# A fused graph-network and feed-forward kernel: the dense stage joined, with router work moved behind the sums and the last evictions on VectorE

## The chip, the core and the metric

The kernel runs on one core of a Trainium2 chip. A core has TensorE (PE in the profile: matrix products, results in PSUM), VectorE (DVE), ScalarE (ACT), GpSimd (POOL) and SyncE (SP, which here issues transfers between HBM and the on-chip SBUF). Each engine takes its own instructions in order; they meet by semaphores. The metric is device time in microseconds (us) of one execution, lower is better.

## The reference, cut to what matters

There are 3125 nodes with 256 features, 50000 edges sorted by destination, and two layers. Each layer is a graph step and a feed-forward step, each on the layer-normed rows, added back. The stage of this case computes the end of the first graph step, the whole first feed-forward step, and the start of the second graph step:

```
# end of graph step 0: agg and denominators are already summed per node
msgs = where(deg > 0, agg, V)                  # 3125 x 256, four heads
y    = msgs @ Wo + bo + h                      # h: the normed node rows
x    = x + layernorm(y) * gamma + beta

# feed-forward step 0, on h = layernorm(x)
weights = h @ wr + br                          # one router weight a node
sel     = the 1561 nodes with the largest weights
z       = gelu(h @ w1 + b1) @ w2 + b2          # 256 -> 1024 -> 256
x       = x + h + (z * weights at sel, 0 elsewhere)

# start of graph step 1
h = layernorm(x);  stored to HBM: h and h @ w_d
```

## The kernel before, in words

The kernel is a chain of stages. `build_dense` is the third of them; in the profiled execution it runs from about 1589 to 2002 us of the span. The nodes lie as 125 partitions by 25 tiles (`P` = 125, `NT` = 25). Five tiles are a group (`G` = 5, `NG` = 5 groups, written g below), and a group is worked in three units of 2, 2 and 1 tiles (written (g, i)). Inside the stage nothing is scheduled by a planner: each engine's order is what its block of code writes, and semaphores (`s_...`) join them.

**Back part (sums of the graph step).** For each group VectorE's `prepare` makes the divided sums (lines 1984, 1986, 1990; each over 125 x 1280 elements). TensorE's `turn_sums` transposes them into the one PSUM bank `ps_t` (line 1705), ScalarE's `turned_sums` copies them out (line 1851), `back_product` multiplies by `wo` (line 1716). ScalarE's `node_rows` writes the normed node rows `nb` (line 1842), GpSimd adds the bias `bo` to them (line 1692), and VectorE's `evict` adds the product (line 2000) and takes statistics (line 2005). Then come `spread`, a square root on ScalarE (`back_root`, line 1857), `back_scales`, the scaling on ScalarE (`back_normalised`, line 1862), and on VectorE `added` (gamma, beta, lines 2033 to 2040), `moments` (line 2063) and, from group 3 on, `normalise(g - 3)` (lines 2083, 2086).

**Router work of a group.** `rank_rows(g)`: TensorE transposes the group's normed rows into the one bank `ps_w` unit by unit (`turn`, line 1730), ScalarE copies each to `h_t` (`turned`, line 1874); TensorE then makes the router weights in two halves of 320 and 305 nodes, again in `ps_w` (`weigh`, line 1743), and ScalarE copies each half to `row` (`weighed`, line 1880). With one bank, each step waits for the copy before it. `rank_rows(0)` and `rank_rows(1)` stand, on TensorE and on ScalarE, behind the first unit of sums of groups 3 and 4, ahead of the other two units.

**Feed-forward part.** `layer1` (line 1756) and ScalarE's `gelu` (line 1888) go through 8 chunks of 128 of the 1024 hidden columns, two halves each; `layer2` (line 1769) goes unit by unit. Four chunks of group 0 stand behind group 3's sums and four behind group 4's. `layer2(0, 0)` stands between `rank_rows(2)` and `rank_rows(3)`, the rest of `layer2(0, ...)` behind `rank_rows(4)`; then groups 1 to 4 follow. VectorE's `own_weights` (2093, 2096), `order` (2103 to 2110: the rank of each tile's weights among all), `biased` (2124), `gates`, `gated` (2132, 2136) run beside it.

**Last part.** For each group: `scales` on VectorE (2151 to 2155), `normalised` on ScalarE (1937), TensorE `turn_back` (1809) into one of two banks, ScalarE `turned_back` (1946), TensorE `spin` (1820: the product with `w_d`) into one of two banks, ScalarE `spun_out` (1955) into one of two pieces of SBUF, SyncE's store (1680). ScalarE's order interleaves these group by group, and the square roots `root_back` (1932) of a group stand directly ahead of its `normalised`.

## Time and profile before

| | us |
|---|---|
| median of 3 runs (lowest to highest) | 3384.34 (3380.32 to 3385.76) |
| the profiled execution's own time | 3386.62 |
| its span | 3384.7 |

| engine | busy us | share of the span |
|---|---|---|
| PE | 2547.7 | 75% |
| DVE | 2239.3 | 66% |
| POOL | 1500.8 | 44% |
| ACT | 1415.8 | 42% |

These shares are means over stages with different limits, so they do not say what bounds the dense stage. That is read from the timeline of the stage, which lists instructions in order of time with the idle time before each, and from busy times by stretch. The name `d_...` marks a tile of this stage; `agg` is the memory that this stage also uses for the normed rows. The trace counts an fp32 matmul as two instructions.

### The profile page before, as it was taken

How to read it: one execution, taken by the hardware profiler on the slowest of the kernel's cores; microseconds unless marked ns; L12 is line 12 of the kernel's file. 1: busy time of each engine (PE TensorE's matmuls, PEld its weight loads, DVE VectorE, ACT ScalarE, POOL GpSimd, SP SyncE). 2: the span in 40 equal slices, each digit the busy share in tenths (PEclk: the TensorE clock that was granted, in tenths of full speed). 3: DMA queues.
4: the chain of work that ended last, by engine and by line, in shares of the span. 5: the costliest groups of instructions: out<-in, count | busy, mean ns of one | idle time of the engine just before them, and what ended most of it. 6: DMA issues, size and time to landing. Idle time of an engine off the chain costs nothing. (4 is left out here: it accounts for less than half of the span.)

```text
span 3384.7 us, 46930 instructions
## 1 busy us (share of the span) xinstructions
PE 2547.7 (75%) x13339; PEld 1901.5 (56%) x13339; DVE 2239.3 (66%) x5226; ACT 1415.8 (42%) x5164; POOL 1500.8 (44%) x1409
## 2 busy tenths in 40 slices
PE   6555666634777777775369957999999969999997
PEld 3434454422444444443246845666666658789997
DVE  8655565525888888886866828999999962022221
ACT  1000000000555555556232237888888841233332
POOL 0566666615555545550100025666666503434442
PEclk9965656655788878887679978999999979999999
DMA  4223232276677767773200046666666652322223
GB/s 111 67 53 88 71 88 76 84 40 193 199 211 223 214 199 217 212 214 97 73 0 1 8 142 180 199 199 197 201 200 201 164 159 84 71 46 39 38 36 65
DMA packets 288291, 419.61 MB, mean 124 GB/s; under 512 B 118887, under 2 KB 200651, under 8 KB 287720
## 3 DMA queue, kind: packets, MB, share of 16 engines
q0 software_dynamic: 91456, 234.61, 24.5%
q1 hardware_dynamic: 167218, 180.43, 20.0%
q10 hardware_dynamic: 29366, 1.56, 0.8%
q8 instruction: 115, 1.88, 0.2%
q14 instruction: 136, 1.11, 0.1%
HBM read 358.58 MB, written 61.03 MB: 124 GB/s over the span
## 5 line engine op out<-in xcount | busy, mean ns | idle before, releaser
L1314 POOL DMA_INDIRECT g_rows<-h_d,src x416 | 452.8, 1088 | 550.5 <-POOLq L74 319.0
L966 POOL DMA_INDIRECT a_strip<-kv_d,src x416 | 402.1, 966 | 423.0 <-DVE x L1109 204.9
L326 POOL DMA_INDIRECT rec_d<-o_rec_in,o_place x392 | 398.0, 1015 | 293.6 <-DVE o_place L554 171.6
L997 ACT ACTIVATE x<-a_strip,x 128x64 f32<-128x64 f32 x1664 | 408.4, 334 | 220.5 <-PE a_psv L1042 165.9
L1042 PE MATMUL a_psv<-x 128*125 128x260 f32 x832 | 316.1, 488 | 170.5 <-issue 90.4
L410 PE MATMUL o_ps_base<-o_run,o_lo_hot_t 125*128 125x26 f32 x782 | 172.2, 374 | 211.5 <-issue 109.1
L1042 PEld LDWEIGHTS a_psv<-x 128*125 128x125 f32 x832 | 156.0, 223 | 258.6 <-issue 135.4
L410 PEld LDWEIGHTS o_ps_base<-o_run,o_lo_hot_t 125*128 125x128 f32 x782 | 160.2, 304 | 221.2 <-issue 114.4
L1412 PE MATMUL g_psa<-g_msg,g_hot 128*125 128x256 f32 x832 | 232.4, 403 | 56.6 <-issue 52.2
L1022 PE MATMUL a_psq<-q,a_ht 125*128 x1248 | 221.7, 339 | 21.5 <-DVE a_ht L1100 15.6
L1412 PEld LDWEIGHTS g_psa<-g_msg,g_hot 128*125 128x125 f32 x832 | 140.1, 188 | 172.8 <-issue 159.3
L1140 DVE TENSOR_TENSOR agg<-agg,a_psv 125x260 f32 x416 | 173.8, 418 | 82.5 <-DMA lo_rows_d<-o_turned_b 49.4
L2472 DVE TENSOR_TENSOR e_w1s<-e_psy,e_room 128x256 f32<-128x256 f32 x56 | 23.8, 424 | 290.4 <-PE e_psy L2675 290.4
L2566 POOL DMA_INDIRECT x_d<-e_w1s,e_listed x56 | 110.0, 1964 | 225.9 <-DVE e_w1s L2474 213.8
L2663 PE MATMUL e_psh<-e_w1s,e_h_t 128*128 128x128 f32 x1792 | 209.3, 275 | 0.0
L2675 PE MATMUL e_psy<-e_w,e_w2s 128*128 x896 | 204.3, 382 | 3.9 <-DMA e_w<-in_L_ffn_W2p 3.9
L2663 PEld LDWEIGHTS e_psh<-e_w1s,e_h_t 128*128 128x128 f32 x1792 | 204.6, 192 | 0.2
L1022 PEld LDWEIGHTS a_psq<-q,a_ht 125*128 125x128 bf16 x1248 | 146.0, 118 | 93.5 <-issue 41.2
L2675 PEld LDWEIGHTS e_psy<-e_w,e_w2s 128*128 128x128 f32 x896 | 167.2, 192 | 24.9 <-issue 4.1
L2745 ACT ACTIVATE e_w2s<-e_psh,e_b 128x128 f32<-128x128 f32 x448 | 128.4, 368 | 121.7 <-PE e_psh L2663 121.6
L1458 DVE TENSOR_TENSOR agg<-agg,g_psa 125x256 f32 x416 | 168.0, 404 | 3.3 <-PE g_psa L1412 2.0
L1358 ACT ACTIVATE g_msg<-g_vec,g_en 128x192 f32<-128x192 f32 x416 | 155.3, 457 | 0.0
(436 smaller groups left out, 5441.5 us busy)
## 6 DMA issues: line engine op xcount, KB each, us to landing
a_row<-rows_d SPq DMA_DIRECT2D x104, 256.0 KB
hot_d<-x SPq DMA_DIRECT2D x104, 250.0 KB
g_hot<-hot_d SPq DMA_DIRECT2D x104, 250.0 KB
o_row<-dst_rows_d SPq DMA_DIRECT2D x98, 256.0 KB
o_row_lo<-lo_rows_d SPq DMA_DIRECT2D x98, 128.0 KB
e_w<-in_L_ffn_W1p SPq DMA_DIRECT2D x8, 1024.0 KB
e_w<-in_L_ffn_W2p SPq DMA_DIRECT2D x8, 1024.0 KB
a_strip<-kv_d,src POOLq DMA_INDIRECT x416
```

The costliest lines, as they stand in the source:

```text
L326: pool.indirect_dma_start(out=m.rec_d[:, :], out_offset=bass.IndirectOffsetOnAxis(ap=place[s % RP][:, u:u + 1], axis=0), in_=rec_in[:, U * ...
L410: last = pe.matmul(ps_base[b][:, u * NH:(u + 1) * NH], lo_hot_t[b][0:P, u, :], table, start=True, stop=True)
L966: pool.indirect_dma_start(out=strip[:, lane.start + u, place:place + 2, :].rearrange("p a d -> p (a d)"), out_offset=None, in_=m.kv_d[:, : ...
L997: act.activation(msg[b][:, u, h, 0:HD], strip[:, lane.start + u, place, h * HD:(h + 1) * HD], ACT.Copy, scale=w[:, k * U + u, h:h + 1])
L1022: last = pe.matmul(ps_q[b][:, u, :], ht[b][0:P, u * EP:(u + 1) * EP], m.q[:, j, k, :], start=k == 0, stop=k == 2)
L1042: pe.matmul(ps_v[u % 2][:, 0:H * HW], hot[b][:, u, :], msg[b][:, u, :, :].rearrange("p h d -> p (h d)"), start=True, stop=True).then_inc(s ...
L1140: dve.tensor_tensor(agg, agg, ps_v[u % 2][:, 0:H * HW], ALU.add).then_inc(s_add, 1)
L1314: pool.indirect_dma_start(out=rows[r][:, u, 64:576], out_offset=None, in_=m.h_d[:, :], in_offset=bass.IndirectOffsetOnAxis(ap=m.src[:, s * ...
L1412: last = pe.matmul(ps_a[k][:, u % 2, :], hot[s % RH][:, u, :], msg[s % RM][:, u, :], start=True, stop=True)
L1458: dve.tensor_tensor(m.agg[:, j, :], m.agg[:, j, :], ps_a[u // 2][:, u % 2, :], ALU.add).then_inc(s_sum, 1)
L2663: last = pe.matmul(ps_h[b][:, c * EP:(c + 1) * EP], own[b][:, k, c * 128:(c + 1) * 128], xt[b][:, k, :], start=k == 0, stop=k == 1)
L2675: last = pe.matmul(ps_y[b][:, 0:D], ht[b][:, c, :], w2[:, e, c, :], start=c == 0, stop=c == NF - 1)
```

## The change

1. `ps_t` and `ps_w` become rings of two banks (banks 6 and 7 are added, which only `layer2` used until then). A transposition may now run ahead of the copy of the one before.
2. `weigh` writes into the two banks of `layer1` instead of `ps_w`. New waits keep the two apart: `weigh` waits for the `gelu` reads before it (`DONE`), `layer1` for the `weighed` reads (`WEIGHED`).
3. `rank_rows(0)` and `rank_rows(1)` stand behind all three units of sums of groups 3 and 4, and on ScalarE behind `back_normalised`.
4. `rank_rows(2)`, `(3)`, `(4)` follow each other; `layer2(0, 0)` is behind all of them.
5. GpSimd's bias addition goes to VectorE (`biases(g)`, ahead of `evict(g)`). GpSimd has no work in the stage.
6. In the last part ScalarE's `spun_out` goes to VectorE, behind all of its other work of the stage, with four pieces of SBUF instead of two. ScalarE does `normalised(0)` and `(1)` first, then stays one group ahead with `normalised`. `scales(0)` to `(3)` stand behind `gated(3)`.

```diff
-        ps_t, ps_o, ps_w, ps_h, ps_y = bank[0], bank[1:3], bank[3], bank[4:6], bank[6:8]
+        ps_t, ps_o, ps_w, ps_h, ps_y = (bank[0], bank[6]), bank[1:3], (bank[3], bank[7]), bank[4:6], bank[6:8]
...
+        DONE = (0, 4, NF, NF, NF)
+        WEIGHED = {(0, 0): 0, (0, 4): 1, (1, 0): 4}
...
-        @block.gpsimd
-        def _(pool):
-            pool.wait_ge(s_c, 64)
-            for g in range(NG):
-                pool.wait_ge(s_n, g + 1)
-                pool.tensor_tensor(nb[g % 2], nb[g % 2], bo[:, None, :].to_broadcast([P, G, D]), ALU.add
-                                   ).then_inc(s_nb, 1)
...
             def turn_sums(g, i):
                 q = UNITS * g + i
                 pe.wait_ge(s_prep, g + 1)
-                if q:
-                    pe.wait_ge(s_ht0, q)
+                if q >= 2:
+                    pe.wait_ge(s_ht0, q - 1)
...
             def turn(g, i):
                 q = UNITS * g + i
                 pe.wait_ge(s_norm, tiles(g, i)[-1] + 1)
-                if q:
-                    pe.wait_ge(s_ht, q)
-                if q and i == 0:
-                    pe.wait_ge(s_row, 2 * g)
+                if q >= 2:
+                    pe.wait_ge(s_ht, q - 1)
...
             def weigh(g, i):
...
-                elif i:
-                    pe.wait_ge(s_row, n)
+                if DONE[g]:
+                    pe.wait_ge(s_g, 2 * DONE[g] - 1 + i)
+                if n >= 2:
+                    pe.wait_ge(s_row, n - 1)
...
             def layer1(g, cs):
...
+                        if (g, c) in WEIGHED:
+                            pe.wait_ge(s_row, 2 * WEIGHED[g, c] + i + 1)
...
-                if g >= 3:
-                    if i == 0:
-                        rank_rows(g - 3)
-                    if i == UNITS - 1:
-                        layer1(0, range(4) if g == 3 else range(4, NF))
-            rank_rows(2)
-            layer2(0, 0)
-            rank_rows(3)
-            rank_rows(4)
-            for i in range(1, UNITS):
+                if g >= 3 and i == UNITS - 1:
+                    rank_rows(g - 3)
+                    layer1(0, range(4) if g == 3 else range(4, NF))
+            for n in range(2, NG):
+                rank_rows(n)
+            pe.wait_ge(s_ht0, UNITS * NG)
+            pe.wait_ge(s_ht, UNITS * NG)
+            for i in range(UNITS):
                 layer2(0, i)
...
-            for g in range(NG):
+            def turned_group(g):
+                for i in range(UNITS):
+                    turned_back(g, i)
+
+            for g in range(NG - 1):
                 root_back(g)
+            normalised(0)
+            normalised(1)
+            turned_group(0)
+            root_back(NG - 1)
+            for g in range(2, NG):
                 normalised(g)
-                turned_back(g, 0)
-                if g:
-                    spun_out(g - 1, 2)
-                turned_back(g, 1)
-                spun_out(g, 0)
-                turned_back(g, 2)
-                spun_out(g, 1)
-            spun_out(NG - 1, 2)
+                turned_group(g - 1)
+            turned_group(NG - 1)
...
+            def spun_out(g, i):
+                q, n = UNITS * g + i, len(tiles(g, i))
+                dve.wait_ge(s_mm3, q + 1)
+                if q >= RS:
+                    dve.wait_ge(s_kept[q % RS], 16 * len(PARTS) * (q // RS))
+                dve.tensor_copy(spun[q % RS][:, 0:n, :], bank[2 + q % 2][0:P, 0:n * D].rearrange("p (n d) -> p n d", d=D)).then_inc(s_spun, 1)
+
+            def biases(g):
+                dve.wait_ge(s_n, g + 1)
+                dve.tensor_tensor(nb[g % 2], nb[g % 2], bo[:, None, :].to_broadcast([P, G, D]), ALU.add
+                                  ).then_inc(s_nb, 1)
```

The order of instructions on TensorE at group 3's sums, before (1705 transposes sums, 1716 multiplies them by `wo`, 1730 and 1743 are `turn` and `weigh` of group 0, 1756 is `layer1`):

```order
L1705 MATMUL d_ps<-ident,d_slot 128x125 x4
L1716 MATMUL d_ps<-d_wo,d_rt 125x256 x4
L1730 MATMUL d_ps<-ident,agg 128x125 x10
L1743 MATMUL d_ps<-d_h_t,d_wr_all 125x320 x2
L1743 MATMUL d_ps<-d_h_t,d_wr_all 125x305 x2
L1705 MATMUL d_ps<-ident,d_slot 128x125 x2
L1716 MATMUL d_ps<-d_wo,d_rt 125x256 x4
L1705 MATMUL d_ps<-ident,d_slot 128x125 x4
L1716 MATMUL d_ps<-d_wo,d_rt 125x256 x2
L1756 MATMUL d_ps<-d_h_t,d_w 128x320 x2
```

The same place in the changed kernel (1700, 1711, 1723, 1738 and 1753 are the same five in that order):

```order
L1700 MATMUL d_ps<-ident,d_slot 128x125 x4
L1711 MATMUL d_ps<-d_wo,d_rt 125x256 x4
L1700 MATMUL d_ps<-ident,d_slot 128x125 x2
L1711 MATMUL d_ps<-d_wo,d_rt 125x256 x4
L1700 MATMUL d_ps<-ident,d_slot 128x125 x4
L1711 MATMUL d_ps<-d_wo,d_rt 125x256 x2
L1723 MATMUL d_ps<-ident,agg 128x125 x10
L1738 MATMUL d_ps<-d_h_t,d_wr_all 125x320 x2
L1738 MATMUL d_ps<-d_h_t,d_wr_all 125x305 x2
L1753 MATMUL d_ps<-d_h_t,d_w 128x320 x2
```

The router work of group 0 has moved from behind the first unit's product to behind the third's.

TensorE again, from the last chunk of group 0's `layer1` to group 1's, before (1769 is `layer2`):

```order
L1756 MATMUL d_ps<-d_h_t,d_w 128x305 x2
L1730 MATMUL d_ps<-ident,agg 128x125 x10
L1743 MATMUL d_ps<-d_h_t,d_wr_all 125x320 x2
L1743 MATMUL d_ps<-d_h_t,d_wr_all 125x305 x2
L1769 MATMUL d_ps<-d_w,d_hs 125x256 x16
L1730 MATMUL d_ps<-ident,agg 128x125 x10
L1743 MATMUL d_ps<-d_h_t,d_wr_all 125x320 x2
L1743 MATMUL d_ps<-d_h_t,d_wr_all 125x305 x2
```

And in the changed kernel (1766 is `layer2`):

```order
L1738 MATMUL d_ps<-d_h_t,d_wr_all 125x305 x2
L1723 MATMUL d_ps<-ident,agg 128x125 x10
L1738 MATMUL d_ps<-d_h_t,d_wr_all 125x320 x2
L1738 MATMUL d_ps<-d_h_t,d_wr_all 125x305 x2
L1766 MATMUL d_ps<-d_w,d_hs 125x256 x40
L1753 MATMUL d_ps<-d_h_t,d_w 128x320 x2
```

All 40 products of `layer2(0, ...)` now stand behind the last group's router work.

ScalarE in the last part, before (1932 root, 1937 `normalised`, 1946 `turned_back`, 1955 `spun_out`):

```order
L1932 ACTIVATE d_rs<-d_rs 125x5
L1937 ACTIVATE agg<-x,d_nmr,d_rs 125x256 x5
L1946 ACTIVATE d_rt<-d_ps 128x500 x2
L1955 ACTIVATE d_slot<-d_ps 125x512
L1946 ACTIVATE d_rt<-d_ps 128x250
L1955 ACTIVATE d_slot<-d_ps 125x512
L1932 ACTIVATE d_rs<-d_rs 125x5
L1937 ACTIVATE agg<-x,d_nmr,d_rs 125x256 x5
```

And in the changed kernel (1926 root, 1931 `normalised`, 1940 `turned_back`):

```order
L1926 ACTIVATE d_rs<-d_rs 125x5 x4
L1931 ACTIVATE agg<-x,d_nmr,d_rs 125x256 x10
L1940 ACTIVATE d_rt<-d_ps 128x500 x2
L1940 ACTIVATE d_rt<-d_ps 128x250
L1926 ACTIVATE d_rs<-d_rs 125x5
L1931 ACTIVATE agg<-x,d_nmr,d_rs 125x256 x5
L1940 ACTIVATE d_rt<-d_ps 128x500 x2
L1940 ACTIVATE d_rt<-d_ps 128x250
```

The copies of the products are gone from ScalarE, and two groups are normalised before the first is transposed.

## Rows read from the trace of the kernel before

**Rows 1.** Busy time by stretch: length, busy (instructions) per engine, PE clock, DMA share, GB/s.

```profile
1627.00:1710.00 83.00, 38.17 (x133) 28.47 (x134) 55.94 (x101) 24.11 (x51) 8.66 (x3) 0.64 0.10 27
1710.00:1760.00 50.00, 32.71 (x115) 22.07 (x113) 33.23 (x78) 22.23 (x42) 0.00 (x0) 0.86 0.00 0
1760.00:1808.00 48.00, 36.91 (x133) 26.40 (x134) 26.25 (x48) 8.85 (x18) 0.00 (x0) 0.79 0.00 1
1808.00:1946.00 138.00, 137.07 (x580) 108.61 (x579) 119.23 (x267) 38.65 (x72) 0.00 (x0) 1.00 0.02 5
1946.00:2003.00 57.00, 36.07 (x151) 28.96 (x149) 7.65 (x32) 25.65 (x54) 0.14 (x1) 0.83 0.35 102
```

**Rows 2.** Timeline, GpSimd's additions beside VectorE: start, duration, engine, line, [idle before, releaser].

```profile
1606.15 8.25 POOL L1692 TENSOR_TENSOR d_room<-d_room,d_bo 125x1280 f32<-125x1280 f32 x2 [79.78 <-DMA d_gamma<-in_L_gnn_gamma]
1607.60 4.07 DVE L1990 TENSOR_TENSOR d_slot<-d_slot,d_room 125x1280 f32<-125x1280 f32 x1
1611.58 4.17 DVE L1984 TENSOR_TENSOR d_room<-d_room,d_dz 125x1280 f32<-125x1280 f32 x1
...
1617.19 1.49 DVE L1990 TENSOR_TENSOR d_slot<-d_slot,d_room 125x1280 f32<-125x1280 f32 x1
...
1640.18 4.05 DVE L1990 TENSOR_TENSOR d_slot<-d_slot,d_room 125x1280 f32<-125x1280 f32 x1
```

**Rows 3.** Timeline, sums of groups 0 to 2.

```profile
1626.96 0.59 ACT L1851 ACTIVATE d_rt<-d_ps 128x500 f32<-128x500 f32 x1 [15.48 <-DVE unit L2057]
1627.69 1.07 PE L1705 MATMUL d_ps<-ident,d_slot 125*128 125x125 f32 x4 [14.88 <-ACT d_rt L1851]
1628.55 3.41 PE L1716 MATMUL d_ps<-d_wo,d_rt 128*125 128x256 f32 x8
...
1665.43 2.57 ACT L1862 ACTIVATE d_room<-d_room,d_nmr,d_rs 125x256 f32<-125x256 f32 x5 [5.05 <-DVE d_nmr L2027]
...
1673.19 0.69 DVE L2000 TENSOR_TENSOR d_room<-d_ps,d_room 125x512 f32<-125x512 f32 x1
```

**Rows 4.** Timeline, groups 3 and 4 with the router work between their units.

```profile
1685.98 2.57 ACT L1862 ACTIVATE d_room<-d_room,d_nmr,d_rs 125x256 f32<-125x256 f32 x5 [5.04 <-DVE d_nmr L2027]
...
1697.11 0.68 DVE L2000 TENSOR_TENSOR d_room<-d_ps,d_room 125x512 f32<-125x512 f32 x1
...
1709.71 0.69 DVE L2000 TENSOR_TENSOR d_room<-d_ps,d_room 125x512 f32<-125x512 f32 x1 [11.13 <-PE d_ps L1716]
...
1714.30 2.57 ACT L1862 ACTIVATE d_room<-d_room,d_nmr,d_rs 125x256 f32<-125x256 f32 x5 [0.78 <-DVE d_nmr L2027]
...
1728.26 0.58 ACT L1851 ACTIVATE d_rt<-d_ps 128x500 f32<-128x500 f32 x1
...
1745.69 2.57 ACT L1862 ACTIVATE d_room<-d_room,d_nmr,d_rs 125x256 f32<-125x256 f32 x5 [0.53 <-DVE d_nmr L2027]
```

**Rows 5.** Timeline, last gelu of group 0, router halves, layer 1 and 2.

```profile
1758.91 0.52 ACT L1888 ACTIVATE d_hs<-d_ps,d_b 128x305 f32<-128x305 f32 x1 [0.50 <-PE d_ps L1756]
...
1767.05 2.50 PE L1743 MATMUL d_ps<-d_h_t,d_wr_all 128*125 128x320 f32 x4 [0.47 <-ACT d_h_t L1874]
...
1784.22 1.34 PE L1743 MATMUL d_ps<-d_h_t,d_wr_all 128*125 128x320 f32 x4 [0.47 <-ACT d_h_t L1874]
...
1808.36 2.27 PE L1756 MATMUL d_ps<-d_h_t,d_w 128*128 128x320 f32 x8
...
1860.50 17.43 PE L1769 MATMUL d_ps<-d_w,d_hs 128*125 128x256 f32 x80
```

**Rows 6.** Timeline, last part of the stage and the start of the next.

```profile
1949.27 1.89 PE L1820 MATMUL d_ps<-w_all,d_rt 128*125 128x256 f32 x8
...
1955.03 0.65 PE L1809 MATMUL d_ps<-ident,agg 125*128 125x125 f32 x4 [3.87 <-ACT agg L1937]
...
1998.34 0.39 ACT L1955 ACTIVATE d_slot<-d_ps 125x256 f32<-125x256 f32 x1 [0.76 <-DMA h_d<-d_slot]
...
2002.21 1.85 SPq L1326 DMA_DIRECT2D g_hot<-hot_d  x4
```

More of the change, by code:

```diff
@@ L1516, in build_dense @@
     RT = 2
+    RS = 4
     A_STEPS, B_STEPS = 5, 4
@@ L2193, in _ @@
                         gated(n)
-                        if n == 1:
-                            scales(0)
+                    for n in range(g):
+                        scales(n)
                 for i in range(UNITS):
@@ L2203, in _ @@
             gated(NG - 1)
-            for g in range(1, NG):
-                scales(g)
+            scales(NG - 1)
+            for unit in units:
+                spun_out(*unit)
 @stage
```

35 lines of the change are left out of this document (14 added, 21 removed).

## The prediction

> **What bounds the stage now.** I first read the busy times by stretch [rows 1]. From 1808 to 1946 us TensorE is busy 137.07 of 138 us at a granted clock of 1.00: there it is the bound, and nothing that the change moves on other engines shortens it. Elsewhere it is not: 38.17 of 83 us (1627 to 1710), 32.71 of 50, 36.91 of 48, and 36.07 of 57 in the last part. VectorE has 55.94 of the first 83 us. So these 238 us are a chain of waits between engines, and the timeline says which. The page's chain of what ended last stays in the final stage of the kernel and says nothing here; I take the later stages to start when this one ends, and to shift with it.
>
> In the sums part [rows 3] the loop of one group is: ScalarE copies the transposed sums (0.59), TensorE transposes the next unit (1.07, of which 0.86 stand ahead of the product), multiplies (3.41 at the lower clock), VectorE evicts and takes statistics, prepares the sums two groups on, makes the scales, ScalarE scales (2.57), and copies again. In group 3 a second wait comes in [rows 4]: VectorE has evicted unit 0 at 1697.11 and then idles 11.13 us until 1709.71, because TensorE does the router work of group 0 between the units. The same again in group 4. In the last part [rows 6] TensorE idles 3.87 us a group for ScalarE's `normalised`, which stands behind the last copy of the group before.
>
> **Startup and GpSimd's addition.** Beside a GpSimd addition VectorE's line 1990 takes 4.05 and 4.07 us, and 1984 takes 4.17; alone, 1990 takes 1.49 [rows 2]. The difference is 2.56 to 2.68. At the start two such instructions follow each other, up to 5.2 us. But the second, at 1611.58, reads a transfer that may not have landed much earlier: at least the 2.7 us of its own stretch go, and I take 3.0 (bounds 2.6 and 5.2). In groups 0, 1 and 2 one `prepare` each gets 2.56 back.
> The Trainium skill (SBUF — State Buffer, section "SBUF: two separate sides") says that the port pair of VectorE and GpSimd is an exclusive lock held for a whole instruction. By that rule all 2.56 us come back; if line 1990 were simply long, none would, and the sum would be about 10 us smaller. The row at 1617.19 stands with the rule.
>
> The added VectorE instruction is of the shape 125x1280 from SBUF, so 1.49 [rows 2]. In groups 0 and 1 it hides behind the product, for which VectorE waits. In groups 2 and 3 VectorE is itself last (its eviction at 1673.19 shows no wait [rows 3]), so it costs 1.49 there; below it could cost nothing if it were covered, above 1.49 each.
>
> **The sums, step by step.** The ring of two takes the 0.86 us of transposition from ahead of the product; I give back 0.5, since TensorE then starts its burst later and the next product meets the lower clock for longer. Group 0: -3.0 - 0.86 + 0.5 - 2.56 = -5.9. Group 1: -0.86 + 0.5 - 2.56, so -8.8, and `back_normalised(1)`, before at 1665.43, comes at 1656.6. Group 2: +1.49 - 0.2 (a wait for the product that goes) - 2.56, so -10.1: `back_normalised(2)` at 1675.9 instead of 1685.98 [rows 4].
> Group 3: from there to the first eviction VectorE has 11.13 us of work of its own (1685.98 to 1697.11), so 1687.0, and with the addition 1688.5. TensorE has all three products by then (2.57 + 0.59 + 3.41 + two more, some 10 us after 1675.9). No 11.13 us wait: first unit 1.47, and from the second eviction to the scaling 4.59 (1709.71 to 1714.30), less some 0.2 of waiting: `back_normalised(3)` at 1694.4, before 1714.30, -19.9.
>
> **Router work and layer 1 of group 0.** It now follows the scaling: 1694.4 + 2.57 = 1697.0. Two copies of 0.59, one of 0.38 and the step of TensorE between them make 1.75. The two router halves stand next to each other without a copy between them: after an idle TensorE the first takes 2.50 (the 1767.05 row of rows 5), the second I take at 2.0. Its copy adds 0.6: 1703.8. Then the table load of 1.28 and eight gelu halves at TensorE's pace: 2.27 us per four pairs, so 1.05 a half [rows 5], 0.6 for the first, 6.3, 0.6 at the end: 1712.6. There the sums of group 4 start, before at 1728.26 [rows 4], -15.7. With all its VectorE work done early and TensorE at the higher clock, two products of 1.89 and 0.4 for a transposition, the evictions and 1.9 for the scales make 9.1: `back_normalised(4)` at 1721.7, before 1745.69, -24.0. The same sequence again (2.6 + 1.75 + 4.7 + 0.6 + 1.3 + 7.5) ends group 0's last gelu at 1740.1, before 1759.4 [rows 5], -19.3.
>
> **Router work of groups 2 to 4.** The two roots and their table load take 1.6, and VectorE's `normalise(3)` and `(4)` are hidden behind group 2's work. A group then costs the copies (0.6 + 0.6 + 0.4 + 0.15), two halves (1.34 + 1.26, at the higher clock [rows 5]) and a copy of 0.6, 4.9 in all: TensorE is through at 1741.7 + 3 x 4.9 - 0.6 = 1755.8. `layer2(0)` is 17.43 whole [rows 5], so group 1's layer 1 starts at 1773.5, before at 1808.36: -34.9. VectorE then waits for `layer2(0, 0)` until 1763 before its first rank; but as before it has two ranks of 4.05 beside the rest of `layer2(0)`, and so the same distance to TensorE as before when group 1 begins. From there to the end of the feed-forward part nothing changes.
>
> **The last part,** in the clock of before. ScalarE does four roots and two `normalised` while TensorE is still in `layer2(4)`. TensorE's own work is 6.2 us a group: two products of 1.89 and half a one, transpositions at 0.65 for a unit [rows 6], some 31 us for five. VectorE is late once: `gated(4)` and `scales(4)` end at about 1952.4, TensorE's third product waits for the first copy and the fourth for `normalised(2)`, 2.6 us in all. Each VectorE copy is bounded by the eviction of the same shape, 0.69 [rows 3]; the copy on ScalarE cost 0.60, so five groups cost VectorE some 9 us of 27, hidden. The end of the last product: 1946 + 31 + 2.6 = 1979.3, of the last copy 1979.9, where before it was 1998.73 [rows 6]: -18.8. The store behind it (to 2002.2) stays.
>
> **Sum:** -34.9 - 18.8 = -53.7; I take off one for new waits of 0.1 us that I have not listed: -53. The profiled execution's own time of 3386.62 becomes 3333.6. It lies 2.3 over the median of 3384.34, and from the median the forecast is 3331.
>
> **Rivals.** (a) *The clock does not hold.* If TensorE has the lower clock in the router work of groups 2 to 4, each half costs 1.16 more (2.50 against 1.34), 7 us for six; gelu's two bursts may lose 2 each, and the last part some 6 of its 31. Time: 3331 + 17 = 3348. For it: 0.64 in the first stretch, 0.79 in the third, 0.83 in the last part [rows 1]. Against: TensorE enters from a full burst, and its gaps get smaller. The Trainium skill (TensorE: Matmul & The Clock Gate, Part 1) says that the throttled clock is the default and that activity releases it; by this rule the denser order keeps 2.4 GHz, where the rows decide only that both levels occur.
> (b) *The last part gains half.* VectorE's copies or the stores (0.35 of the transfer engines before, about 0.6 afterwards) set the pace, say 8 us a group: 18.8 becomes 10. Time 3340.
> (c) *VectorE's ranking is the bound.* Its 119.23 of 138 us [rows 1] leave 19 us; if the ranks start later against TensorE than I say, the front gain is given back beside layer 2. With all of it lost only -18.8 stays: 3366. With the last part's gain lost too, no change. Against: the first rank depends on the same product as TensorE's next step.
> (d) *Slower.* VectorE works in order, and eleven of its fifteen copies wait for the store of the copy four before. If a store's round trip is L, a unit takes L/4 instead of 2.1 us; the last part of now 57 us plus the 35 gained earlier are eaten when 15 units take over 85 us, at L = 23. At L = 25 the kernel is at 3393. Against: before, with a ring of two, the last copy waited 0.76 us [rows 6].
> (e) *It does not do what it says:* a copy or wait left in place keeps the units apart. The order of the instructions speaks against it.
>
> **How the numbers follow.** Forecast 70%, its own range 3324 to 3340. (a) 14%, (b) 8%, (c) 3%, (d) 2%, (e) or nothing 3%. A gain larger than the forecast is possible too: 2.2 more at the start, 2 to 4 if the clock is high where I took it low. The range 3320 to 3352 holds the forecast, (a) and (b). A measurement can tell 0.2%, 6.8 us, from no change: faster by more 95%, within 3%, slower 2%.
>
> **What the profile of the changed kernel would show.** No idle time of about 11 us ahead of VectorE's second eviction in group 3; line 1990's successor at 1.49 throughout; group 1's layer 1 some 35 us earlier; TensorE busy over 0.85 of the last part, and that part about 38 us instead of 57. It would be wrong if TensorE waits for VectorE's copies in each group of the last part, if the router halves of groups 2 to 4 take over 2 us each, or if the dense stretch of 138 us shows idle time.

## The result, and the profile after

The changed kernel takes 3322.47 us (median of 4 runs, 3318.29 to 3330.13), the kernel before 3382.33 beside it (3377.04 to 3385.76): ratio 0.9827, 95% interval 0.9803 to 0.9851. That is 59.9 us less, where 53 were forecast (3331, range 3320 to 3352). The time lies in the stated range, but 1.5 us below the narrower one of 3324 to 3340 that the forecast itself had.

The profiled execution took 3319.88 us, 66.7 less than that of before. Not all of it is the change: ScalarE's first scaling of the stage, which the change does not touch, comes at 1590.68 after 1598.93 before, so 8.25 us lie ahead of the stage. From there to the first transfer of the next stage it is 403.28 us before and 343.41 after: 59.9 less, the same as the medians say. From here on "+" before a time of the stage means that it is counted from that first scaling. A step's gain is its time before, less its time after plus 8.25.

Busy time by stretch, in the stretches that answer to those of before [rows 1] (columns as there):

```profile
1618.75:1701.75 83.00, 41.88 (x164) 31.60 (x162) 68.06 (x140) 30.43 (x65) 0.00 (x0) 0.73 0.10 27
1701.75:1740.00 38.25, 27.91 (x110) 19.50 (x109) 32.65 (x72) 19.37 (x38) 0.00 (x0) 0.87 0.00 0
1740.00:1762.00 22.00, 21.19 (x101) 17.75 (x100) 13.10 (x18) 2.92 (x6) 0.00 (x0) 1.00 0.00 1
1762.00:1900.00 138.00, 137.07 (x582) 108.78 (x581) 121.09 (x280) 41.51 (x80) 0.00 (x0) 1.00 0.02 5
1900.00:1935.00 35.00, 27.79 (x147) 22.98 (x145) 14.30 (x35) 14.88 (x31) 0.27 (x1) 0.98 0.57 165
```

The dense stretch is what it was: 137.07 of 138 us. The last part is 35 us instead of 57, with TensorE busy 0.79 of it and the transfer engines 0.57. TensorE's busy time for the same work falls there as well, from 36.07 to 27.79 us, and the granted clock up to its last product rises from 0.84 to 1.00: some 8 of the 22 us are TensorE's clock, and the rest is waiting.

Timeline of the changed kernel, sums (start, duration, engine, line, then idle time before and its releaser), answering to rows 2 and 3:

```profile
1602.13 1.49 DVE L1973 TENSOR_TENSOR d_room<-d_room,d_dz 125x1280 f32<-125x1280 f32 x1 [1.29 <-DMA d_room<-kv_d]
1605.06 1.49 DVE L1979 TENSOR_TENSOR d_slot<-d_slot,d_room 125x1280 f32<-125x1280 f32 x1
...
1647.31 2.57 ACT L1857 ACTIVATE d_room<-d_room,d_nmr,d_rs 125x256 f32<-125x256 f32 x5 [2.50 <-DVE d_nmr L2016]
1655.07 1.49 DVE L2156 TENSOR_TENSOR d_room<-d_room,d_bo 125x1280 f32<-125x1280 f32 x1
1656.60 0.69 DVE L1989 TENSOR_TENSOR d_room<-d_ps,d_room 125x512 f32<-125x512 f32 x1
```

Groups 3 and 4, answering to rows 4:

```profile
1679.08 0.69 DVE L1989 TENSOR_TENSOR d_room<-d_ps,d_room 125x512 f32<-125x512 f32 x1
1680.47 0.68 DVE L1989 TENSOR_TENSOR d_room<-d_ps,d_room 125x512 f32<-125x512 f32 x1
1684.58 2.58 ACT L1857 ACTIVATE d_room<-d_room,d_nmr,d_rs 125x256 f32<-125x256 f32 x5 [0.53 <-DVE d_nmr L2016]
1687.77 0.65 PE L1723 MATMUL d_ps<-ident,agg 125*128 125x125 f32 x2 [5.32 <-ACT d_h_t L1869]
1688.89 3.58 PE L1738 MATMUL d_ps<-d_h_t,d_wr_all 128*125 128x320 f32 x8 [0.47 <-ACT d_h_t L1869]
...
1704.71 0.69 DVE L1989 TENSOR_TENSOR d_room<-d_ps,d_room 125x512 f32<-125x512 f32 x1 [7.51 <-PE d_ps L1711]
```

The eviction of unit 1 follows that of unit 0 after 1.4 us; the idle 11.13 us are gone. But TensorE now idles 5.32 us ahead of the third transposition of the router work (5.65 in group 4), because ScalarE's copies stand behind its five scalings at 1684.58, and after it the eight router instructions take 3.58 (granted clock 0.65).

Router work of groups 2 and 4, layers, answering to rows 5:

```profile
1730.99 0.41 PE L1723 MATMUL d_ps<-ident,agg 125*128 125x125 f32 x2 [1.93 <-ACT d_h_t L1869]
1731.86 4.06 PE L1738 MATMUL d_ps<-d_h_t,d_wr_all 128*125 128x320 f32 x8 [0.47 <-ACT d_h_t L1869]
...
1742.44 2.37 PE L1738 MATMUL d_ps<-d_h_t,d_wr_all 128*125 128x320 f32 x8 [0.47 <-ACT d_h_t L1869]
1744.64 17.43 PE L1766 MATMUL d_ps<-d_w,d_hs 128*125 128x256 f32 x80
...
1752.22 0.69 DVE L2113 TENSOR_TENSOR agg<-d_ps,d_b 125x512 f32<-125x512 f32 x1 [5.17 <-PE d_ps L1766]
```

Last part, answering to rows 6:

```profile
1906.54 1.10 PE L1815 MATMUL d_ps<-w_all,d_rt 128*125 128x256 f32 x4 [1.40 <-DVE d_slot L2152]
...
1910.57 2.55 ACT L1931 ACTIVATE agg<-x,d_nmr,d_rs 125x256 f32<-125x256 f32 x5
...
1916.17 2.55 ACT L1931 ACTIVATE agg<-x,d_nmr,d_rs 125x256 f32<-125x256 f32 x5
...
1929.48 0.42 DVE L2152 COPY d_slot<-d_ps 125x256 f32<-125x256 f32 x1 [0.17 <-PE d_ps L1815]
1934.09 1.77 SPq L1326 DMA_DIRECT2D g_hot<-hot_d  x4
```

A group takes 5.60 us (1910.57 to 1916.17). TensorE is busy for all of them and ScalarE for 3.89. TensorE waits for a VectorE copy once, 1.40 us.

### The profile page after: what moved, and what is told of

Its sections match the earlier page's. It is cut to its first block and busy times, and to the rows that moved or that the text cites. A ratio compares the mean times of both kernels' runs of the same rounds, so it can differ in the third digit from the quotient of the medians.

```text
span 3318.0 us, 46937 instructions
## 1 busy us (share of the span) xinstructions
PE 2517.3 (76%) x13339; PEld 1883.0 (57%) x13339; DVE 2245.1 (68%) x5246; ACT 1406.5 (42%) x5149; POOL 1489.7 (45%) x1404
## 5 line engine op out<-in xcount | busy, mean ns | idle before, releaser
L373 ACT ACTIVATE q<-o_qf 125x256 bf16<-125x256 f32 x75 | 31.0, 414 | 297.8 <-DVE o_qf L622 209.1
```

## The experiments

The executions ran on several occasions, where the kernel before took 3420.76, 3191.35, 3190.58 and 3382.80 us (the second and the last under the same chip number, so it is not the chip alone). Most of that difference lies ahead of this stage. So each kernel is read by its ratio to the kernel before that ran beside it, and by the stage in its own trace. The first is too coarse for a few us. The second repeats well: where the code is the same, `back_normalised(2)` starts at +75.45 to +77.28, so a difference of less than 2 us over the whole stage tells nothing. Behind the layers it repeats better still: from layer 1 of group 1 to the next stage the nine kernels with the new last part and the same code there take 172.16 to 172.29 us, and the two with the old one 193.85 (before) and 193.78 (u_tail). What concerns the last part alone is therefore read from that stretch.

| kernel | ratio (95%) | `back_normalised(2)` | `back_normalised(4)` | last gelu, group 0 | layer 1, group 1 | next stage | against changed |
|---|---|---|---|---|---|---|---|
| before | 1 | 87.05 | 146.76 | 160.50 | 209.43 | 403.28 | +59.9 |
| forecast | | 77.0 | 122.8 | 141.2 | 174.5 | 350.3 | +6.9 |
| changed | 0.9827 (0.9803 to 0.9851) | 75.75 | 120.02 | 138.08 | 171.23 | 343.41 | 0 |
| u_bias | 0.9835 (0.9818 to 0.9853) | 85.96 | 129.51 | 147.83 | 180.98 | 353.14 | +9.7 |
| u_rank | 0.9870 (0.9854 to 0.9887) | 76.42 | 127.37 | 140.84 | 177.84 | 350.09 | +6.7 |
| u_ring | 0.9889 (0.9873 to 0.9906) | 76.05 | 124.60 | 146.06 | 197.69 | 369.89 | +26.5 |
| u_tail | 0.9889 (0.9871 to 0.9906) | 75.79 | 121.09 | 138.59 | 171.67 | 365.45 | +22.0 |
| b_tail | 0.9927 (0.9906 to 0.9948) | 86.88 | 146.48 | 160.25 | 209.20 | 381.37 | +38.0 |
| t_order | 0.9827 (0.9810 to 0.9843) | 76.62 | 120.98 | 139.06 | 172.21 | 349.48 | +6.1 |
| t_act | 0.9831 (0.9813 to 0.9848) | 76.83 | 121.25 | 139.38 | 172.53 | 350.46 | +7.1 |
| u_rs2 | 0.9818 (0.9802 to 0.9834) | 75.61 | 120.91 | 138.40 | 171.48 | 347.52 | +4.1 |
| best1 | 0.9807 (0.9790 to 0.9823) | 76.80 | 127.24 | 140.51 | 173.35 | 345.64 | +2.2 |
| best3a | 0.9785 (0.9763 to 0.9807) | 75.45 | 118.72 | 126.01 | 166.51 | 338.67 | -4.7 |
| best3c | 0.9807 (0.9779 to 0.9835) | 75.78 | 119.05 | 126.34 | 164.95 | 337.20 | -6.2 |
| best3b | 0.9768 (0.9747 to 0.9788) | 77.28 | 117.94 | 125.23 | 156.60 | 328.81 | -14.6 |

(Starts in us from ScalarE's first scaling; of the gelu its end; where `back_normalised(4)` is spread out, its first instruction.)

### u_bias: the bias on GpSimd again

```diff
+        @block.gpsimd
+        def _(pool):
+            pool.wait_ge(s_c, 64)
...
             for g in range(NG):
-                biases(g)
                 evict(g)
```

> The changed kernel with one part undone: the five additions of the bias to the group's rows go back to GpSimd. All else stays. Theory (the additions cost VectorE, because VectorE's own long operation runs beside them at 4.05 us in place of 1.49): the dense stage is 8.6 us longer than in the changed kernel (3.9 at its start, two times 2.56 and once 1.07 behind it, less the 1.49 that VectorE no longer spends on the fifth), so about 51 us under the kernel before, and the line that adds to the rows shows 4.05 us again where it lies beside GpSimd. Rival (the long line is long by itself, and the change only shifted who adds): the stage is as long as in the changed kernel or up to 3 us shorter, since VectorE has five additions of 1.49 less.

Timeline of this kernel at the start of the stage:

```profile
1638.96 8.31 POOL L1695 TENSOR_TENSOR d_room<-d_room,d_bo 125x1280 f32<-125x1280 f32 x2 [83.01 <-DMA d_gamma<-in_L_gnn_gamma]
...
1640.46 4.07 DVE L1987 TENSOR_TENSOR d_slot<-d_slot,d_room 125x1280 f32<-125x1280 f32 x1
1644.45 4.17 DVE L1981 TENSOR_TENSOR d_room<-d_room,d_dz 125x1280 f32<-125x1280 f32 x1
...
1650.07 1.49 DVE L1987 TENSOR_TENSOR d_slot<-d_slot,d_room 125x1280 f32<-125x1280 f32 x1
```

The same line takes 4.07 us beside GpSimd's addition and 1.49 alone, and the stage is 9.7 us longer; the rival forecast 0 to 3 shorter. The Trainium skill (SBUF — State Buffer, section "SBUF: two separate sides") gives the two engines one port pair, locked for a whole instruction. Putting the addition back brought both the durations and the loss, and so this trace agrees.

### u_rank: the router work of groups 0 and 1 ahead of the units again

```diff
-                if g >= 3 and i == UNITS - 1:
-                    rank_rows(g - 3)
-                    layer1(0, range(4) if g == 3 else range(4, NF))
+                if g >= 3:
+                    if i == 0:
+                        rank_rows(g - 3)
+                    if i == UNITS - 1:
+                        layer1(0, range(4) if g == 3 else range(4, NF))
```

(and the same on ScalarE)

> The changed kernel with one part undone: the router work of groups 0 and 1 stands again behind the first unit of groups 3 and 4, on TensorE and ScalarE. The rings of two, the router's own banks and all else stay. Theory A (the prediction's step: the place sets the end, because VectorE's second eviction waits 11 us behind it): 10 us or more longer in each of the groups 3 and 4 up to back_normalised, and 8 to 20 us longer in all. Theory B (formed from the trace after: in the changed kernel TensorE stands idle 5.3 and 5.7 us in each of the two groups because ScalarE's copies of the turned rows stand behind back_normalised, and the router halves then run at the lower clock; the place only moves the same work from before the gelu to before the eviction): back_normalised comes 5 to 8 us later in each, the gelu comes right behind it, and the stage is 0 to 2 us longer, so 58 to 60 us under the kernel before.

Timeline of the kernel before: its router work begins.

```profile
1694.75 0.65 PE L1730 MATMUL d_ps<-ident,agg 125*128 125x125 f32 x4 [1.33 <-DVE agg L2083]
```

Timeline of this kernel: the same place and the two evictions of group 3, the second eviction of group 4, and TensorE behind the last gelu:

```profile
1709.04 2.52 PE L1723 MATMUL d_ps<-ident,agg 125*128 125x125 f32 x10 [1.92 <-DVE agg L2075]
1712.91 0.69 DVE L1992 TENSOR_TENSOR d_room<-d_ps,d_room 125x512 f32<-125x512 f32 x1
...
1719.02 0.69 DVE L1992 TENSOR_TENSOR d_room<-d_ps,d_room 125x512 f32<-125x512 f32 x1 [4.63 <-PE d_ps L1711]
...
1747.06 0.69 DVE L1992 TENSOR_TENSOR d_room<-d_ps,d_room 125x512 f32<-125x512 f32 x1 [5.94 <-PE d_ps L1711]
...
1767.75 2.52 PE L1723 MATMUL d_ps<-ident,agg 125*128 125x125 f32 x10 [3.62 <-DVE agg L2075]
1770.74 4.53 PE L1738 MATMUL d_ps<-d_h_t,d_wr_all 128*125 128x320 f32 x8 [0.47 <-ACT d_h_t L1871]
```

Neither theory holds. With rings and banks of its own the router work makes the second eviction wait 4.63 and 5.94 us, where it waited 11.13 and 8.60 before. Not all of group 3's 6.5 us are the banks'. From the start of the router work to the second eviction it is 9.98 us here (1709.04 to 1719.02) and 14.96 before (1694.75 to 1709.71): 5.0 us come from TensorE's side, its clock with them (the product of that unit takes 1.99 us here and 3.62 before). The other 1.5 are VectorE's, whose first eviction now stands behind the added instruction (3.87 us after the start of the router work, 2.36 before). Without them the wait would be 6.1 us here. So undone in this order the place has some 6 of the 11.13 us, and the rings and the router's own banks have 5. Up to the last gelu B is nearly right (+2.8). What B left out comes behind it: VectorE's chain started 7.4 us late in group 4, so TensorE waits 3.62 us for the normed rows of group 2, and then has the lower clock (the router work takes 4.53 us at a granted clock of 0.50). Together 6.7.

### u_ring: one bank each again

```diff
-        ps_t, ps_o, ps_w, ps_h, ps_y = (bank[0], bank[6]), bank[1:3], (bank[3], bank[7]), bank[4:6], bank[6:8]
+        ps_t, ps_o, ps_w, ps_h, ps_y = bank[0], bank[1:3], bank[3], bank[4:6], bank[6:8]
...
-                if q >= 2:
-                    pe.wait_ge(s_ht, q - 1)
+                if q:
+                    pe.wait_ge(s_ht, q)
```

> The changed kernel with two parts undone: one bank each for the turned sums and the turned rows in place of rings of two, and the router's product in the bank of the turned rows, with the waits of the kernel before. The place of the router work behind its units stays. Theory: the three groups of router work behind the gelu lose their 4.4 us each again and take about 9.5 (some 15 us), the two ahead of it 2 to 4 us each, and the units of the first three groups 0 to 3 in all: 15 to 24 us longer, 36 to 45 under the kernel before. Rival (most of what was gained there was the clock, that would hold without rings as well): 5 to 8 us longer.

Timeline of this kernel, router work of group 3:

```profile
1777.71 1.06 PE L1725 MATMUL d_ps<-ident,agg 125*128 125x125 f32 x4 [0.70 <-ACT d_row L1873]
1779.54 1.07 PE L1725 MATMUL d_ps<-ident,agg 125*128 125x125 f32 x4 [0.77 <-ACT d_h_t L1867]
1781.38 0.65 PE L1725 MATMUL d_ps<-ident,agg 125*128 125x125 f32 x2 [0.77 <-ACT d_h_t L1867]
1782.50 2.50 PE L1738 MATMUL d_ps<-d_h_t,d_wr_all 128*125 128x320 f32 x4 [0.47 <-ACT d_h_t L1867]
1785.71 2.37 PE L1738 MATMUL d_ps<-d_h_t,d_wr_all 128*125 128x305 f32 x4 [0.71 <-ACT d_row L1873]
1788.77 1.06 PE L1725 MATMUL d_ps<-ident,agg 125*128 125x125 f32 x4 [0.70 <-ACT d_row L1873]
```

26.5 us, over the 24 of the theory and far from the rival. Group 3 takes 11.06 us (1777.71 to the next at 1788.77) and group 4 10.16 up to layer 2, against 4.44 each in the changed kernel, and group 2 takes 4.5 more than there: 16.8 us. I had 15, from 9.5 a group, since before groups 3 and 4 of the router work came behind a burst of layer 2 and had the higher clock (1.34 a half [rows 5]); here they never get out of the lower one (granted 0.50 over the whole of group 3). Groups 0 and 1 cost 8.0, the upper end, and layer 2 of group 0 begins in the lower clock, 1.7. Each step waits only 0.5 to 0.8 us, but the router's eight instructions take 4.87 instead of 2.37. The units of sums gain almost nothing from their ring (+0.3 at `back_normalised(2)`). This is the largest part of the change. Of the 6.6 us of group 3, 2.5 are slower router instructions and 1.3 slower transpositions: more than half is the clock. How much of it is the ring of the turned rows and how much the router's own banks was not separated. The parts undone in u_bias, u_rank, u_ring and u_tail come to 64.9 us, 5.0 more than the whole. That may be overlap, or no more than the 2 us that each reading leaves open.

### u_tail and b_tail: the last part alone

u_tail puts into the changed kernel the last part of before; b_tail puts the new one into the kernel before. ScalarE's order in b_tail (the ring of four, VectorE's copies and the early scales go with it and are left out here):

```diff
...
+            for g in range(NG - 1):
                 root_back(g)
+            normalised(0)
+            normalised(1)
+            turned_group(0)
+            root_back(NG - 1)
+            for g in range(2, NG):
+                normalised(g)
+                turned_group(g - 1)
+            turned_group(NG - 1)
```

> The changed kernel with the last part of the dense stage as before: ScalarE evicts the projected rows between its copies of the turned ones, the pieces go round in a ring of two, and the scales of groups 1 to 3 are worked out behind the last group's rows. Theory: 21.7 us longer (what the two traces differ by there), the rest of the stage the same to 1 us. Rival (part of the 21.7 came from the stage's earlier part, through clock or a DMA queue): less than 18 us.

> The kernel before with the last part of the dense stage alone changed (normalisations one group ahead on ScalarE, VectorE evicting the projected rows in a ring of four, scales of four groups worked out ahead). Theory: the last part is worth what it was worth undone, 22 us shorter than the kernel before, since TensorE is free and hot when it begins in both. Rival (it leans on what the front gives, VectorE being through with its work sooner): 15 us or less, with VectorE's scales or copies late.

22.0 us are lost in the one and 21.9 won in the other. From layer 1 of group 1 on it is 21.6 and 21.7, so nearly all of it lies behind the layers. The last part is worth the same with either front.

### t_order and t_act: ScalarE's order, and the engine that evicts

t_order has ScalarE's old order and VectorE's copies. t_act has the new order, and ScalarE copies (the first diff is t_order, the second t_act, where the moved `spun_out` and its last call are left out):

```diff
-            normalised(0)
-            normalised(1)
-            turned_group(0)
-            root_back(NG - 1)
-            for g in range(2, NG):
+            for g in range(NG):
+                if g == 1:
+                    root_back(NG - 1)
                 normalised(g)
-                turned_group(g - 1)
-            turned_group(NG - 1)
+                turned_group(g)
```
```diff
             def turned_group(g):
                 for i in range(UNITS):
                     turned_back(g, i)
+                    if g or i:
+                        spun_out(*units[UNITS * g + i - 1])
...
```

> The changed kernel, with ScalarE's order in the last part as before: each group's five normalisations stand right ahead of its own three copies of turned rows (the root of group 4 ahead of group 1). VectorE goes on evicting the projected rows, in a ring of four. Theory (the order, that lets TensorE turn a group's first rows while ScalarE normalises the next, is worth about as much as the other engine): by the durations of the trace after a group takes 2.55 + 0.6 + 1.0 + 0.6 + 1.9 + 0.3 + 0.2 + 0.4, some 7.4 us in place of 5.6, so 7 us longer over four groups (5 to 9). Rival (taking the copies off ScalarE is what counts, the order only follows from it): 0 to 2 us longer.

> The changed kernel, with ScalarE evicting the projected rows again: its new order of normalisations one group ahead stays, and behind each copy of turned rows stands the copy of the unit before. VectorE has none; the ring of four stays. Theory: ScalarE's work of a group grows from 4.1 to 5.7 us and it waits for TensorE ahead of two of the copies, so a group takes some 7.9 us in place of 5.6: 9 us longer over four groups (7 to 12). Rival (the engine makes no difference once the order is right): 0 to 3 us longer, a group at the 5.7 us of ScalarE's work.

Timeline of t_order, one group on ScalarE, and TensorE waiting behind it:

```profile
1738.25 2.55 ACT L1931 ACTIVATE agg<-x,d_nmr,d_rs 125x256 f32<-125x256 f32 x5
1740.86 0.65 PE L1804 MATMUL d_ps<-ident,agg 125*128 125x125 f32 x4 [1.19 <-ACT agg L1931]
...
1745.05 2.56 ACT L1931 ACTIVATE agg<-x,d_nmr,d_rs 125x256 f32<-125x256 f32 x5
```

Timeline of t_act:

```profile
1744.95 0.60 ACT L1949 ACTIVATE d_slot<-d_ps 125x512 f32<-125x512 f32 x1 [2.40 <-PE d_ps L1815]
```

The whole stage is 6.1 and 7.1 us longer, but 1.0 and 1.3 of that had come by layer 1 of group 1, where the code is the same. Behind it they are 5.1 and 5.8. So t_order's theory holds (5 to 9; a group takes 6.8 us where 7.4 were expected). t_act's lies short of its 7 to 12: ScalarE's scalings of groups 2, 3 and 4 are 7.55 and 9.22 us apart, near the 7.9 expected, but only these two intervals are stretched and not four. With either half undone some three quarters of the 21.6 us stay, so neither rival holds and neither half alone explains the gain. u_tail undoes both, and the ring of four and the early scales as well. The two halves and the ring (u_rs2, below: 3.9) come to 14.8 one by one. The 6.8 that are left are the late scales, or halves that cover for each other; no run separates these.

### u_rs2: pieces in a ring of two

```diff
-    RS = 4
+    RS = 2
...
-        spun = [slot[0][:, 0:2, :], slot[0][:, 2:4, :], slot[1][:, 0:2, :], slot[1][:, 2:4, :]]
+        spun = [slot[0][:, 0:2, :], slot[0][:, 2:4, :]]
```

> The changed kernel, with the projected rows' pieces in a ring of two in place of four. All else stays. Theory: a copy then waits for the store of two units ago, 3.7 us back at the rate of the trace after; the stores take about that, so 0 to 3 us longer, and the same within what can be told is likely. Rival (the prediction's slower case in small: the store's round trip sets the pace of the last part): 8 us or more longer, with VectorE's copies waiting for DMA.

```profile
1732.02 0.69 DVE L2152 COPY d_slot<-d_ps 125x512 f32<-125x512 f32 x1 [0.80 <-PE d_ps L1815]
...
1737.19 0.42 DVE L2152 COPY d_slot<-d_ps 125x256 f32<-125x256 f32 x1 [2.56 <-DMA h_d<-d_slot]
```

(Timeline, VectorE in the last part.) 4.1 us longer (3.9 of them behind the layers), more than the 0 to 3 I gave it, less than the rival's 8. The mechanism is the rival's: nine copies wait for a store. The piece whose copy ends at 1732.71 is free again at 1737.19, a round trip of 4.5 us; in the nine it is 2.5 to 5.0. Two units at the new pace give 3.7. With four pieces there are 7.5 us for it, and no copy waits.

### best1: ScalarE's router copies ahead of the scaling

```diff
-                back_normalised(g)
                 if g >= 3:
                     rank_rows(g - 3)
+                if g != 3:
+                    back_normalised(g)
+                if g >= 3:
                     gelu(0, range(4) if g == 3 else range(4, NF))
+                if g == 3:
+                    back_normalised(3)
```

> The changed kernel with ScalarE's order altered in the groups 3 and 4: its copies of the router work come ahead of the normalisation back_normalised(4), and back_normalised(3) goes behind the first gelu burst. All else stays. Theory A (TensorE's 5.3 and 5.7 us of idleness ahead of the third turn lie on the path, and the router halves are slow because of them): 4 to 5 us gained in group 3; in group 4 the next group's normalise on VectorE is ready only some 1 us sooner than TensorE asks for it now, so there up to 1 us of it stays: 5 to 6 us shorter than the changed kernel in all. Theory B (both idles stay hidden behind VectorE's chain, as the run with the router work in its old place showed that chain to matter): 0 to 2 us shorter. Theory C (both idles are paid): 9 us or more shorter.

Timeline of this kernel, TensorE:

```profile
1527.68 3.68 PE L1711 MATMUL d_ps<-d_wo,d_rt 128*125 128x256 f32 x8 [3.10 <-ACT d_rt L1846]
...
1547.15 8.27 PE L1753 MATMUL d_ps<-d_h_t,d_w 128*128 128x320 f32 x24 [2.79 <-ACT d_hs L1883]
```

No gain: +2.2, of which 1.0 lies ahead of the altered place. That is nearest to B's sum but not by B's reason. The 2.55 us of scaling had only been put elsewhere on the same path: ahead of the copy of the next unit (TensorE idles 3.10, and the product takes 3.68 instead of 1.99) and ahead of the gelus (2.79, and a burst of 8.27 instead of 6.58).

### best3a, best3b, best3c: the scaling between the gelus, then VectorE and TensorE too

In the gelu burst ScalarE waits 0.50 to 0.56 us ahead of each gelu for TensorE, and one instruction of the scaling fits there. best3a:

```diff
                 turned_sums(g, 2)
+                if g >= 3:
+                    for i in range(UNITS):
+                        turned(g - 3, i)
                 back_root(g)
...
+                    for i in range(2):
+                        weighed(g - 3, i)
+                    gelu(0, range(4) if g == 3 else range(4, NF), between=g)
```

> The changed kernel with ScalarE's order altered in the groups 3 and 4 in another way: the three copies of turned rows come ahead of the two roots (where ScalarE stood idle), the router's two additions behind the roots, and the five normalisations of back_normalised go one by one between the gelus, where ScalarE waits for TensorE half of the time. VectorE and TensorE keep their order. Theory: in group 3 TensorE's idle 5.3 us ahead of the third turn go, and 2.6 of ScalarE's time ahead of the gelus with them, about 8 us, less what the clock takes; in group 4 the same is gained ahead of the gelus, but TensorE then waits for VectorE's normalise of group 2, which comes only as much sooner as group 3 gave: 6 to 9 us shorter than the changed kernel. Rival (as in the run before, whatever is moved comes back as a wait ahead of the next unit or as a lower clock): 0 to 3 us shorter.

```profile
1542.41 2.52 PE L1723 MATMUL d_ps<-ident,agg 125*128 125x125 f32 x10 [7.15 <-DVE agg L2089]
1545.40 4.53 PE L1738 MATMUL d_ps<-d_h_t,d_wr_all 128*125 128x320 f32 x8 [0.47 <-ACT d_h_t L1873]
```

(Timeline of best3a, TensorE behind the last gelu.) The gelus end 12.1 us sooner, but only 4.7 reach the end, between the theory's 6 to 9 and the rival's 0 to 3. TensorE waits 7.15 us for VectorE's normed rows and then has the lower clock (granted 0.50 in both rows). The theory had named this wait, without a size. best3b moves VectorE too (TensorE first, then VectorE; ScalarE's root of group 4 is left out):

```diff
-            for n in range(2, NG):
-                rank_rows(n)
+            rank_rows(2)
+            rank_rows(3)
             pe.wait_ge(s_ht0, UNITS * NG)
+            layer2(0, 0)
+            rank_rows(NG - 1)
...
                 back_scales(g)
+                if g == NG - 1:
+                    normalise(2)
                 if g:
                     added(g - 1)
                     moments(g - 1)
+            normalise(3)
             added(NG - 1)
             moments(NG - 1)
-            for g in range(2, NG):
-                normalise(g)
+            normalise(NG - 1)
```

> As the run before of this call, and: VectorE normalises group 2 ahead of adding up group 3, and group 3 ahead of adding up group 4; ScalarE takes the root of group 4 behind the router work of group 3; TensorE computes the first unit of group 0's second layer ahead of the router work of group 4. Theory: TensorE no longer waits for VectorE's chain behind the gelus, and group 1's first layer starts 12 to 18 us sooner than in the changed kernel; VectorE begins to rank 8 to 9 us sooner and has 17 us to spare in the layers, so the end moves by as much: 10 to 16 us shorter than the changed kernel. Rival (VectorE's ranking becomes the bound once TensorE is ahead): 5 to 9 us shorter, with TensorE waiting for VectorE's evictions in the layers.

Timeline of best3b, TensorE:

```profile
1502.85 2.37 PE L1738 MATMUL d_ps<-d_h_t,d_wr_all 128*125 128x320 f32 x8 [0.47 <-ACT d_h_t L1875]
...
1536.28 0.40 PE L1723 MATMUL d_ps<-ident,agg 125*128 125x125 f32 x2 [1.84 <-ACT d_h_t L1875]
1537.15 2.37 PE L1738 MATMUL d_ps<-d_h_t,d_wr_all 128*125 128x320 f32 x8 [0.47 <-ACT d_h_t L1875]
```

14.6 us shorter than the changed kernel, within the theory's 10 to 16. The ratio of 0.9768 is the lowest of all (74 us under the kernel before that ran beside it, where the changed kernel has 59.9). best3c puts that unit of layer 2 back:

> As best3b, but with the first unit of group 0's second layer behind the router work of group 4, where the changed kernel has it. What remains of the difference to the changed kernel is ScalarE's order and VectorE's. In the trace of best3b TensorE is through with group 3's router work at 1543.81 and VectorE's normalise of group 4 gives the first rows some 4 us later. Theory: TensorE waits 3 to 4.5 us there, and one router half meets the lower clock for another 1 to 2: the stage is 4 to 6 us longer than in best3b, 9 to 11 shorter than in the changed kernel. Rival (the place of that unit is what brought the gain over best3a): 9 us or more longer than best3b. Second rival (the wait is hidden by VectorE, which ends the same work at the same time): 0 to 1 us.

Timeline of best3c, TensorE:

```profile
1681.01 4.36 PE L1738 MATMUL d_ps<-d_h_t,d_wr_all 128*125 128x320 f32 x8 [0.47 <-ACT d_h_t L1874]
...
1728.15 2.07 PE L1723 MATMUL d_ps<-ident,agg 125*128 125x125 f32 x10 [4.03 <-DVE agg L2091]
1730.69 4.53 PE L1738 MATMUL d_ps<-d_h_t,d_wr_all 128*125 128x320 f32 x8 [0.47 <-ACT d_h_t L1874]
1735.02 18.06 PE L1766 MATMUL d_ps<-d_w,d_hs 128*125 128x256 f32 x80
```

8.4 us longer than best3b, between the theory's 4 to 6 and the rival's 9. The wait is as forecast, 4.03. Behind it the ten transpositions take 0.65 us more than the 1.42 of best3b, the router work 2.16 more, layer 2 0.63 more than the 17.43 of the changed kernel: 3.4 us of clock on top of 4.0 of waiting. From the last gelu to layer 1 of group 1 that makes 38.6 us instead of 31.4, and these 7.2 are what the place of the unit is worth. The last 1.1 had been lost by the last gelu already, in the router work of group 0 (4.36 us in the first row, 2.37 in best3b's). There the two kernels and best3a (4.47) have the same code and nearly the same waits (TensorE had idled 3.48 us in best3b, 3.79 and 3.73 in the others), so this part is the clock of one execution and not a merit of best3b.

## Why the prediction was right, point by point

The gains of the stage up to each point, forecast and measured in the clock of before:

| up to | forecast | measured |
|---|---|---|
| first copy of sums | -3.0 | -3.9 |
| `back_normalised(1)` | -8.8 | -9.9 |
| `back_normalised(2)` | -10.1 | -11.3 |
| `back_normalised(3)` | -19.9 | -21.5 |
| sums of group 4 | -15.7 | -18.1 |
| `back_normalised(4)` | -24.0 | -26.7 |
| last gelu of group 0 | -19.3 | -22.4 |
| layer 1 of group 1 | -34.9 | -38.2 |
| last part, by itself | -18.8 | -21.7 |
| stage | -53.7 | -59.9 |

- **Startup and GpSimd.** Right, and by its mechanism (u_bias). The second `prepare` does wait for its transfer, 1.29 us at 1602.13, as the prediction had it. 0.9 us more came back than the 3.0 taken.
- **The added instruction** takes 1.49 us, and is last on VectorE in groups 2 and 3 (no wait ahead of the evictions at 1656.60 and 1679.08), as said.
- **Groups 3 and 4.** The 11.13 us wait is gone and the times are right to 1.6 and 2.7 us. But the prediction put the wait down to the place of the router work alone, and said that group 4 has the same one, where it is 8.60 us. By u_rank it was the place and the single banks together: with the place alone put back, 4.63 us of it come back, and 6.1 would if VectorE had not been given its addition. And TensorE does not have all three products before VectorE's first eviction. The third waits 3.7 us behind it, which costs nothing.
- **Router work and gelu.** The two halves took 3.58 and 4.17 us in groups 0 and 1, forecast 4.5 and 4.7; from the scaling of group 3 to the sums of group 4 it is 17.4 us, forecast 18.2. Groups 3 and 4 take 4.44 us each, forecast 4.9, but group 2's halves have the lower clock (4.06 us together, granted 0.58), which takes that back: from the last gelu to group 1's layer 1 it is 33.15 us, forecast 33.4. Over 2 us a half was a sign I had named of being wrong. Group 2 just reaches it, so here the sum is right because two errors largely cancel.
- **The dense stretch** is unchanged, 137.07 of 138 us, and VectorE has room: rival (c) is out. Its own wait of 5.17 us for `layer2(0, 0)` is where the prediction put it.
- **The last part.** TensorE's work of a group was mis-sized: I added 6.2 us from single rows whose times overlap, and it is 5.6, at which TensorE itself sets the pace (busy 5.60 of 5.60 us). Over the part it is busy 27.8 us where I had 31, and the waits forecast at 2.6 us are 1.40. Against that stand some 0.7 of small waits, and 0.7 behind the last copy (4.2 us to the next stage, before 3.5). That leaves 2.9 us. The forecast holds the gain from the clock without a term for it, since its 1.89 and 0.65 us are rows at the higher level. TensorE busy over 0.85 of that part was a sign I had named: it is 0.79 of the 35 us, and 0.94 up to its last product at 1929.4.
- **Rivals.** (a) is there in small and is hidden in the sum: the lower clock in the router work of group 2, not in 3 and 4. (b) is out: 21.7, not 10. (d) has a real round trip of at most 5.0 us (u_rs2), a fifth of what it needed.

- **The sums themselves.** 1755.8 + 17.43 is 1773.2 and not 1773.5, and 1946 + 31 + 2.6 is 1979.6 and not 1979.3. The two slips cancel in the sum. The "one" taken off for new waits was 0.7.

So the mechanism held in the main, with the single banks left out of the wait in group 3, and the miss of 6.9 us is of size: 0.9 at the start, 2.4 in small parts from there to the layers, 2.9 in the last part and 0.7 that I took off for waits that did not come.

What stays open: how the 11.13 us of before split exactly between place and bank, since u_rank and u_ring were not run together; what the early scales are worth; and what point 4 of the change does by itself. That point was never undone alone, and best3b, which puts `layer2(0, 0)` ahead of the router work of group 4 again, suggests that it is not always a gain. Whether best3b gains another us or two from a second unit of layer 2 ahead was not tried.

## What to carry to other kernels

Price a wait of TensorE by the wait and by what the instructions behind it lose to the clock. In best3c the second (3.4 us) was nearly as large as the first (4.0). When work is moved off one engine's path, follow it to the next place where it stands on a path (best1), and look for the engine's idle slots instead: the gelu burst had one of 0.5 us at each step, and five scalings went in for nothing (best3a). Then the next engine's order has to follow, or the gain ends in a new wait (7.15 us), as it did until VectorE's was changed as well.

## What the runs showed of the hardware that was not expected

- Nearly the same gap can cost much or nothing. TensorE idles 1.93 and 0.47 us ahead of the router work of group 2 in the changed kernel, and it takes 4.06 us (granted 0.58). In best3b and best3c it idles 1.84 and 0.47 at the same place, and it takes 2.37 (granted 1.00 in best3b). The changed kernel had idled 5.65 us and had slow router work some 17 us earlier, with a burst at the higher level between. best3b had waited at most 0.65 us at a time for 35 us. That this history is the cause is not shown: the router work of group 0 took 2.37 us in best3b, 4.36 in best3c and 4.47 in best3a, with the same code ahead of it.
- Eight router instructions take 2.37 us at the higher level of 2.4 GHz (granted 1.00, changed kernel) and 4.53 at the lower of 1.2 (granted 0.50, best3a).
- The store of a piece of 125 x 512 elements holds its buffer for 2.5 to 5.0 us from the end of the copy into it (the waits of u_rs2).
- Identity and Copy run between gelus and behind a square root without a table load in the trace; only the switch between gelu and square root has one, 1.28 us, and the next instruction starts right behind it.
